# Sums over values for two heads in one TensorE stream, in a decoder layer on one core

## The chip, the core and the metric

The kernel runs on one core of one Trainium2 chip. A core has TensorE (PE: matmuls and transposes; its weight loads are shown as PEld), VectorE (DVE), ScalarE (ACT), GpSimd (POOL) and SyncE (SP, which here issues the DMA transfers). The metric is the device time of one execution in microseconds (us), lower is better.

## The reference

A decoder layer on x of 2 batches x 512 tokens x 1024. First, attention with 32 query heads, 8 key and value heads, head size 128, and a causal window of 128 keys; then a second mixing step with a quantised context of 2 x 1024 x 1024; then a feed-forward part with ternary weights. Each is added to x and normalised. The part that the change touches:

```python
def _gqa_swa_attention(q, k, v, slide):            # slide = 128
    qg = q.reshape(B, Hkv, G, N, D)                # G = 4 query heads for one k, v head
    s = jnp.einsum('bhgnd,bhmd->bhgnm', qg, k) * scale
    mask = (j <= i) & (i - j < slide)
    p = jax.nn.softmax(jnp.where(mask, s, -inf), axis=-1)
    return jnp.einsum('bhgnm,bhmd->bhgnd', p, v)   # the sums over values
...
o = attention(q, k, v); return o @ wo.T
```
and of the second step the quantised context: `clip(round(ctx / s + z), 0, 255)`.

## The kernel before, in words

All engines run hand-written streams, tied by semaphores. The first 437 us make q, k and v by fp32 products from pairs of values (high and low part, F32R), with three matmuls for each product: high by high, high by low, low by high. Then comes the **attention stage**, from 437 to 1031 us. It has 64 **units**: unit (g, j) is group g (0 to 7, one k and v head), batch j // 4 and query head j % 4, so a group has 8 units, j = 0 to 7. Work goes in **slots**, one for each unit. In slot j every engine runs its `slot_of(g, j)`:

- PE: `scores` of unit j; half of an output product (`out_slot(.., 0, ..)`, 12 matmuls of 512 columns); `values` of unit j - 2; `turn_probs` of unit j - 1 (transposes of the probabilities through PSUM bank 4, `turn_ps`); the second output product. At the end of slots 0 and 4 `turn_values` transposes the values of a batch, through the same bank.
- ACT: copies scores out of PSUM, `query_high` for the next unit, the exponentials, `sums_high(j - 2)` (the sums out of PSUM, rounded to the high part), `probs_high(j - 1)` (the same for the transposed probabilities), and once a slot `make_tile`, which prepares a weight tile of the feed-forward part.
- DVE: `softmax_bias(j)`, the add of the first output product, `check_tile`, `normalise(j)`, `sums_low(j - 2)`, `probs_low(j - 1)`, the add of the second output product.
- POOL: `query_low(j + 1)`, then `mask_probs(j - 1)`: four instructions that write the masked probabilities `pm_h` and `pm_l`, which `values` reads two PE slots after the unit's own.
- SP: loads of q, k, v, output weights, tiles and context, in program order.

A window of 128 keys means that key block a (128 keys) serves query blocks a and a + 1. So `values` has for each a three matmuls of 256 columns, and of 128 for the last block: 12 in a unit. They accumulate in one bank, `o_ps` (bank 5), with the weights `v_h`, `v_l`. Four banks (`y_ps`: 0, 1, 6, 7) take the output products in turn.

`contexts(g, j, ...)` says in which slots a context tile is scaled (ACT, line 1556), rounded (DVE, line 2477) and quantised (ACT, line 1562, in the next slot). The raw tile has two buffers in `ctx_raw`. After the last slot a tail follows: `out_tile`, sums of the context, a normalisation of eight row tiles, then the feed-forward part from about 1100 us.

Of the kernel before, what the change touches and what calls it, by code (L numbers as in the profile page):

```python
# [15 lines left out]
P = 128  # L16
# [8 lines left out]
KCTX = 1024  # L25
# [45 lines left out]
def build(nc, x_rows, x_cols, w_att, ctx_rows, x1_scale, x1_zp, x2_scale, x2_zp, w_gu, w_down, out):  # L71
    with ExitStack() as stack:
# [57 lines left out]
        pm_h = place("pm_h", [P, TPB, 2, P], F32R)  # L130
        pm_l = place("pm_l", [P, TPB, 2, P], F32R)
# [34 lines left out]
        ctx_raw = place("ctx_raw", [P, 2, KCTX], F32, at_r4 + 32768)  # L166
# [79 lines left out]
        y_ps = [bank(0), bank(1), bank(6), bank(7)]  # L246
# [277 lines left out]
        def out_block(j, k, last):  # L524
# [5 lines left out]
            return 0, 0, 2 * (j - 6) + k, 0  # L530

# [149 lines left out]
        def _(sp):  # L681
# [103 lines left out]
            def load_context(k, odd):  # L785
                if isinstance(k, int):
                    wait(sp, ctx_quant, k - 1)
                sp.dma_start(ctx_raw[:, odd, :], ctx_rows[k]).then_inc(ctx_loaded[odd], 16)

            def slot(g, j, first, last):  # L790
# [20 lines left out]
                if not first and j in (0, 2):  # L811
                    if last:
                        for odd in range(2):
                            load_context(2 * (HKV - 2) + j + odd, odd)
                    else:
                        load_context(g * 2 + (j // 2 - 2), j // 2)
# [153 lines left out]
        def _(pe):  # L970
# [79 lines left out]
            def values(g, j):  # L1050
# [5 lines left out]
                for a in range(TPB):  # L1056
# [4 lines left out]
                    ph = pm_h[:, a, 0:wide, :]  # L1061
                    pl = pm_l[:, a, 0:wide, :]
# [4 lines left out]
                last.then_inc(pv_done, 1)  # L1067

# [7 lines left out]
            def out_product(m, into, t, half):  # L1076

                wait(pe, y_added, m - 3)
# [9 lines left out]
            def out_slot(g, j, k, last):  # L1088
# [12 lines left out]
                out_product(g * 16 + (2 * j + k - 12), y_ps[(2 * j + k) % 4], t, half)  # L1101

            def out_tile(t):
# [3 lines left out]
                for half in range(NH):  # L1107
                    m = OUT_BLOCKS - 2 * (TILES - t) + half
                    pe.wait_ge(y_added, m - 1)
                    out_product(m, y_ps[2 + half], t, half)  # L1110

            def slot_of(g, j, first, last):
                early = first and j < 6
                scores(g, j)
                if early:
# [10 lines left out]
                if j % GROUP == 0:  # L1126
                    turn_values(g, j // GROUP)
# [98 lines left out]
            values(g, 6)  # L1226
# [4 lines left out]
            values(g, 7)  # L1231
# [201 lines left out]
        def _(act):  # L1433
# [95 lines left out]

            def head_high(n, e):  # L1530
# [22 lines left out]
            def scale_context(k, odd, loads):  # L1553

                act.wait_ge(ctx_loaded[odd], loads * 16)
                act.activation(ctx_raw[:, odd, :], ctx_raw[:, odd, :], ACT.Relu,
# [1503 lines left out]
```

## Time and profile before

| | |
|---|---|
| median of 3 runs | 1482.17 us (1480.92 to 1483.05) |
| profiled execution, whole | 1483.74 us |
| its span, first to last instruction | 1481.6 us |
| PE busy in the span | 1439.5 us (97%) |
| DVE / ACT / POOL busy | 984.0 / 788.8 / 739.9 us |
| PE busy, 437 to 1031 us (attention) | 586.57 of 594 us |
| granted TensorE clock in that stretch | 1.00 |

The span is the profiler's; the whole is the device time of the same execution, 2.1 us more. PE matmuls overlap: the time that one takes of the engine is the distance between its start and the next one's, not its own duration.

### The profile page before, as it was taken

The numbers are of one execution on the slowest core, as the hardware profiler recorded it, in microseconds if no ns is written. First come the engines' busy times: TensorE is split into PE (matmuls) and PEld (weight loads), VectorE is DVE, ScalarE is ACT, GpSimd is POOL, SyncE is SP. The second block draws the span as 40 slices with busy tenths as digits, with TensorE's granted clock in tenths as the row PEclk, the third lists the DMA queues.
The fourth block names the chain that finished last, engine by engine and source line by source line (L and its number), as shares of the span: only waits on it lengthen the run. The fifth ranks groups of instructions, "written<-read, shape, count | busy, mean of one in ns | idle before, by whom it ended". The sixth has DMA issues, their size and how long they took to land.

```text
span 1481.6 us, 23450 instructions
## 1 busy us (share of the span) xinstructions
PE 1439.5 (97%) x7349; PEld 1174.3 (79%) x7349; DVE 984.0 (66%) x1768; ACT 788.8 (53%) x1561; POOL 739.9 (50%) x651
## 2 busy tenths in 40 slices
PE   8899999999999999999999999999989999999996
PEld 6688888888888888888888888887757887777643
DVE  7644444445556578777777877787776665566587
ACT  5433333333445465656565756674576555555674
POOL 0477777776566455555555455553475434433100
PEclk9999999999999999999999999999999999999999
DMA  6477777877662857575757676772041222222611
GB/s 227 156 273 272 275 283 283 281 275 256 222 222 79 300 184 263 179 272 191 279 184 262 216 244 227 248 230 98 16 156 71 93 86 78 90 92 85 228 43 73
DMA packets 105883, 281.12 MB, mean 190 GB/s; under 512 B 12768, under 2 KB 13152, under 8 KB 105824
## 3 DMA queue, kind: packets, MB, share of 16 engines
q1 hardware_dynamic: 105824, 280.41, 53.9%
q8 instruction: 28, 0.46, 0.1%
q14 instruction: 31, 0.25, 0.1%
HBM read 184.94 MB, written 95.42 MB: 189 GB/s over the span
## 4 chain that ended last, share of the span: by engine, by line
PE 52%; DVE 7%; ACT 3%; DMA 3%; issue 3%; POOL 2%; SPq 1%; DVEq 0%; ACTq 0%; POOLq 0%
PE ps L1083 7%; PE ps L1084 7%; PE ps L1085 7%; PE ps L1246 6%; PE ps L1247 6%; PE ps L1299 5%; PE ps L1034 2%; PE ps L1035 2%; PE ps L1036 2%; PE ps L1065 2%; PE ps L1066 2%; PE ps L1047 2%; PE ps L1064 1%; PE ps L1168 1%; DVE u_val L2761 1%
## 5 line engine op out<-in xcount | busy, mean ns | idle before, releaser
L1015 PE MATMUL ps<-xo_h,wb_h 128*128 128x512 f32 x644 | 251.4, 390 | 6.5 <-DVE xo_l L2323 2.8
L1016 PE MATMUL ps<-xo_l,wb_h 128*128 128x512 f32 x644 | 250.7, 389 | 0.0
L1017 PE MATMUL ps<-xo_h,wb_l 128*128 128x512 f32 x644 | 250.6, 389 | 0.0
L2098 POOL TENSOR_TENSOR pm_l<-pt_l,upto 128x512 fp32r<-128x512 f32 x64 | 82.4, 1288 | 251.8 <-DVE pt_l L2422 251.8
L1083 PE MATMUL ps<-wo_h,o_h 128*128 128x512 f32 x512 | 206.4, 403 | 0.0
L1084 PE MATMUL ps<-wo_l,o_h 128*128 128x512 f32 x512 | 199.8, 390 | 0.0
L1085 PE MATMUL ps<-wo_h,o_l 128*128 128x512 f32 x512 | 199.6, 390 | 0.0
L1459 ACT ACTIVATE wb_h<-wf_l 128x512 fp32r<-128x512 f32 x69 | 43.6, 632 | 197.1 <-DVE wf_l L2351 81.7
L1015 PEld LDWEIGHTS ps<-xo_h,wb_h 128*128 128x128 f32 x644 | 120.9, 188 | 34.6 <-issue 5.9
L2071 POOL TENSOR_TENSOR wb_l<-wf_l,wb_h 128x512 fp32r<-128x512 f32 x66 | 87.7, 1329 | 112.0 <-DVE s_sum L2346 56.6
L1508 ACT ACTIVATE prob<-prob,exp_bias 128x128 f32<-128x128 f32 x256 | 99.8, 391 | 78.4 <-DVE exp_bias L2409 78.4
L1017 PEld LDWEIGHTS ps<-xo_h,wb_l 128*128 128x128 f32 x644 | 120.9, 188 | 25.2
L1016 PEld LDWEIGHTS ps<-xo_l,wb_h 128*128 128x128 f32 x644 | 120.9, 188 | 24.5
L2071 POOL TENSOR_TENSOR wb_l<-raw,wb_h 128x512 fp32r<-128x512 f32 x66 | 89.0, 1349 | 62.1 <-DVE wb_l L2335 47.5
L2432 DVE TENSOR_TENSOR resid<-ps,resid 128x512 f32<-128x512 f32 x128 | 88.3, 690 | 47.3 <-PE ps L1085 43.0
L1085 PEld LDWEIGHTS ps<-wo_h,o_l 128*128 128x128 f32 x512 | 96.1, 188 | 21.3
L1083 PEld LDWEIGHTS ps<-wo_h,o_h 128*128 128x128 f32 x512 | 96.5, 188 | 16.6
L1084 PEld LDWEIGHTS ps<-wo_l,o_h 128*128 128x128 f32 x512 | 96.6, 189 | 15.8
L2087 POOL TENSOR_TENSOR q_l<-q_raw,q_h 128x512 fp32r<-128x512 f32 x64 | 83.6, 1307 | 21.5 <-ACT q_h L1486 21.5
L1246 PE MATMUL ps<-t_h,ws 128*128 128x512 f32 x228 | 88.7, 389 | 0.0
L1247 PE MATMUL ps<-t_l,ws 128*128 128x512 f32 x228 | 88.7, 389 | 0.0
L2082 POOL TENSOR_TENSOR wp_l<-wp_raw,wp_h 128x1024 fp32r<-128x1024 f32 x32 | 76.8, 2399 | 0.0
(252 smaller groups left out, 3649.8 us busy)
## 6 DMA issues: line engine op xcount, KB each, us to landing
raw<-w_att SPq DMA_DIRECT2D x47, 512.0 KB, 5.6
f_raw<-w_gu SPq DMA_DIRECT2D x44, 512.0 KB, 4.8
u_gu<-f_unit SPq DMA_DIRECT2D x42, 512.0 KB, 4.4
gq<-u_gu SPq DMA_DIRECT2D x42, 512.0 KB, 3.7
wp_raw<-w_att SPq DMA_DIRECT2D x32, 512.0 KB, 5.7
wo_high<-wp_h SPq DMA_DIRECT2D x32, 512.0 KB, 2.9
wo_low<-wp_l SPq DMA_DIRECT2D x32, 512.0 KB, 4.2
q_rows<-c SPq DMA_DIRECT2D x64, 256.0 KB, 2.7
```

What stands on the lines that cost most here:

```text
L1015: pe.matmul(prod_ps[i], wh, chunk(xo_h[i], c), start=(i in OPENS and c == 0), stop=False, skip_group_check=True)
L1016: pe.matmul(prod_ps[i], wh, chunk(xo_l[i], c), start=False, stop=False, skip_group_check=True)
L1017: last = pe.matmul(prod_ps[i], wl, chunk(xo_h[i], c), start=False, stop=(c == KH - 1), skip_group_check=True)
L1083: pe.matmul(into, oh, wo_h[half][:, h, :], start=(h == 0), stop=False)
L1084: pe.matmul(into, oh, wo_l[half][:, h, :], start=False, stop=False)
L1085: last = pe.matmul(into, ol, wo_h[half][:, h, :], start=False, stop=(h == GROUP - 1))
L1246: pe.matmul(dst, w[:, c * P:(c + 1) * P], chunk(xh, c), start=(start and c == 0), stop=False, skip_group_check=True)
L1247: last = pe.matmul(dst, w[:, c * P:(c + 1) * P], chunk(xl, c), start=False, stop=(c == KH - 1), skip_group_check=True)
L1508: last = act.activation(prob[:, par, a, :], prob[:, par, a, :], ACT.Exp, bias=exp_bias[:, par, a:a + 1], scale=SCALE, accum_out=row_sum[:, ...
L2071: pool.tensor_tensor(wb_l[i][:, :], weight_source(odd, i), plain(wb_h[i][:, :]), ALU.subtract).then_inc(w_low, 1)
L2087: pool.tensor_tensor(q_l[:, j % 2, :], q_raw[:, :], plain(q_h[:, j % 2, :]), ALU.subtract).then_inc(q_low, 1)
L2432: dve.tensor_tensor(resid[:, t, cols], source, resid[:, t, cols], ALU.add).then_inc(y_added, 1)
```

## The change

`values` is kept for the first six units of group 0. From then on `values_pair(g, j - 3)` runs in odd slots alone and does units j - 3 and j - 2 (always two heads of one batch, with the same values) with one set of weights: one matmul streams the masked probabilities of both heads. The pair's sums need two banks, 5 and 1 (`oq_ps`, each 2 heads x 256 columns). So the output products have three banks in turn instead of four. `pm_h` and `pm_l` get room for two units. `sums_high_pair` and `sums_low_pair` take the two banks one after another, 2 x 256 columns each. `turn_values` moves from the end of slots 0 and 4 to behind the scores of slots 1 and 5, and `value_high` and `value_low` with it. `ctx_raw` has one buffer, whose next load waits for the quantising of the tile before; in the last group the four context tiles go to slots 1, 3, 5, 7 instead of 1 to 4. In the tail `values(g, 6)` and `values(g, 7)` become one `values_pair(g, 6)` at the later place.

```diff
+        oq_ps = [bank(i).rearrange("p (h k) -> p h k", h=2) for i in (5, 1)]
+        y_ps = [bank(0), bank(6), bank(7)]
+        Y_BANK = (0, 1, 2, 0, 1, 2, 0, 1, 2, 0, 1, 2, 0, 1, 2, 1)
...
-            if last and 1 <= j <= 4:
-                k = 2 * (HKV - 2) + j - 1
+            if last and j > 0 and j % 2 == 1:
+                k = 2 * (HKV - 2) + j // 2
...
             def load_context(k, odd):
-                if isinstance(k, int):
-                    wait(sp, ctx_quant, k - 1)
-                sp.dma_start(ctx_raw[:, odd, :], ctx_rows[k]).then_inc(ctx_loaded[odd], 16)
+                wait(sp, ctx_quant, k)
+                sp.dma_start(ctx_raw[:, :], ctx_rows[k]).then_inc(ctx_loaded[odd], 16)
...
+            def values_pair(g, j):
+                n = g * UNITS + j
+                par, b, h = unit(j)
+                pe.wait_ge(p_masked, n + 2)
+                wait(pe, o_low, n)
+                def into(dst, a, first, wide, start, stop):
+                    vh = v_h[b][:, a, :]
+                    vl = v_l[b][:, a, :]
+                    ph = pm_h[:, :, a, first:first + wide, :]
+                    pl = pm_l[:, :, a, first:first + wide, :]
+                    pe.matmul(dst, vh, ph, start=start, stop=False, skip_group_check=True)
+                    pe.matmul(dst, vh, pl, start=False, stop=False, skip_group_check=True)
+                    return pe.matmul(dst, vl, ph, start=False, stop=stop, skip_group_check=True)
+                low, high = oq_ps
+                into(low[:, :, 0:2 * P], 0, 0, 2, True, False)
+                into(low[:, :, P:2 * P], 1, 0, 1, False, True).then_inc(pv_done, 1)
+                into(high[:, :, 0:P], 1, 1, 1, True, False)
+                into(high[:, :, 0:2 * P], 2, 0, 2, False, False)
+                into(high[:, :, P:2 * P], 3, 0, 1, False, True).then_inc(pv_done, 1)
...
                 scores(g, j)
+                if j % GROUP == 1:
+                    turn_values(g, j // GROUP)
...
-                if not first or j >= 2:
+                if first and j >= 2:
                     values(g, j - 2)
+                if not first and j % 2 == 1:
+                    values_pair(g, j - 3)
...
-                if j % GROUP == 0:
-                    turn_values(g, j // GROUP)
...
+            def sums_high_pair(g, j):
...
+                for i in range(2):
+                    act.wait_ge(pv_done, n + (i + 1))
+                    act.activation(o_h[b][:, h:h + 2, i * 2 * P:(i + 1) * 2 * P], oq_ps[i], ACT.Copy).then_inc(o_high, 1)
```

The order in which the instructions stand shows three places. First, PE, the sums over values in a slot of the last group before the change, the end of one unit's (line 1064 to 1066 are high by high, low by high, high by low) and the transposes of the probabilities:

```order
L1064 MATMUL ps<-pm_h,v_h_81 128x256
L1065 MATMUL ps<-pm_l,v_h_81 128x256
L1066 MATMUL ps<-pm_h,v_l_82 128x256
L1064 MATMUL ps<-pm_h,v_h_81 128x128
L1065 MATMUL ps<-pm_l,v_h_81 128x128
L1066 MATMUL ps<-pm_h,v_l_82 128x128
L1047 MATMUL ps<-ident,prob 128x128 x4
```
and of the changed kernel the beginning of a pair's in an odd slot (three more of 128x2x128 follow, then the transposes; 128x2x128 is a stream of 256 columns in two pieces):

```order
L1094 MATMUL ps<-pm_h,v_h_81 128x512
L1095 MATMUL ps<-pm_l,v_h_81 128x512
L1096 MATMUL ps<-pm_h,v_l_82 128x512
L1094 MATMUL ps<-pm_h,v_h_81 128x2x128
L1095 MATMUL ps<-pm_l,v_h_81 128x2x128
L1096 MATMUL ps<-pm_h,v_l_82 128x2x128
L1094 MATMUL ps<-pm_h,v_h_81 128x2x128
L1095 MATMUL ps<-pm_l,v_h_81 128x2x128
L1096 MATMUL ps<-pm_h,v_l_82 128x2x128
L1094 MATMUL ps<-pm_h,v_h_81 128x512
L1095 MATMUL ps<-pm_l,v_h_81 128x512
L1096 MATMUL ps<-pm_h,v_l_82 128x512
```
A pair has 15 matmuls (6 of 512 columns, 9 of 256) where two units had 24 (18 of 256, 6 of 128), and an even slot has none.

Second, PE at the border of slots 4 and 5, before:

```order
L1084 MATMUL ps<-wo_l_155,o_h_149 128x512
L1085 MATMUL ps<-wo_h_153,o_l_151 128x512
L1070 REGISTER_ALU
L1073 MATMUL ps<-ident,v_raw 128x128 x4
L1024 REGISTER_ALU
L1034 MATMUL ps<-k_h_143,q_h 128x128
```
and now, in slot 5:

```order
L1047 MATMUL ps<-k_h_142,q_h 128x256
L1048 MATMUL ps<-k_l_143,q_h 128x256
L1049 MATMUL ps<-k_h_142,q_l 128x256
L1106 REGISTER_ALU
L1109 MATMUL ps<-ident,v_raw 128x128 x4
L68 REGISTER_ALU
L1118 MATMUL ps<-wo_h_152,o_h_148 128x512
```
The transposes of the values moved from ahead of the scores to behind them.

Third, DVE in slot 5 of the last group, before:

```order
L2407 TENSOR_REDUCE row_max<-prob 128x4
L2409 TENSOR_SCALAR exp_bias<-row_max 128x4
L2432 TENSOR_TENSOR resid<-ps,resid 128x512
L2461 TENSOR_TENSOR misfits<-misfits 128x1
L2471 SCALAR_TENSOR_TENSOR f_raw_161,misfits<-f_unit_165,prm,f_raw_161 128x1024
L2415 RECIPROCAL row_inv<-row_sum 128x4
L2417 TENSOR_TENSOR prob<-prob,row_inv 128x512
L2427 TENSOR_TENSOR o_l_151<-ps,o_h_149 128x512
L2422 TENSOR_TENSOR pt_l<-ps,pt_h 128x512
L2432 TENSOR_TENSOR resid<-ps,resid 128x512
```
and now:

```order
L2465 TENSOR_REDUCE row_max<-prob 128x4
L2467 TENSOR_SCALAR exp_bias<-row_max 128x4
L2452 TENSOR_TENSOR v_l_145<-ps,v_h_144 128x512
L2499 TENSOR_TENSOR resid<-ps,resid 128x512
L2528 TENSOR_TENSOR misfits<-misfits 128x1
L2538 SCALAR_TENSOR_TENSOR f_raw_162,misfits<-f_unit_166,prm,f_raw_162 128x1024
L2473 RECIPROCAL row_inv<-row_sum 128x4
L2475 TENSOR_TENSOR prob<-prob,row_inv 128x512
L2493 TENSOR_TENSOR o_l_149<-ps,o_h_147 128x2x256 x2
L2480 TENSOR_TENSOR pt_l<-ps,pt_h 128x512
L2499 TENSOR_TENSOR resid<-ps,resid 128x512
```
The low part of the values came into this slot, and the odd slot has both takings of the sums; the even slots have none ahead of `pt_l`.

## Rows read from the trace of the kernel before

**Rows 1.** Page, part 1: busy time, share, instructions of PE.
```profile
PE 1439.5 (97%) x7349; PEld 1174.3 (79%) x7349; DVE 984.0 (66%) x1768; ACT 788.8 (53%) x1561; POOL 739.9 (50%) x651
```

**Rows 2.** Windows, attention stage: length, busy PE, PEld, DVE, ACT, POOL; clock, DMA, GB/s.
```profile
437.00:1031.00 594.00, 586.57 (x3478) 515.41 (x3477) 449.41 (x885) 355.02 (x903) 308.86 (x345) 1.00 0.63 218
```

**Rows 3.** Waits of PE, 456 to 1031 us: total, times, longest.
```profile
PE ps L1073 <- DVE pt_l L2422: 4.7, 5, 1.6
PE ps L1034 <- POOL q_l L2087: 0.8, 1, 0.8
PE ps L1064 <- POOL pm_l L2103: 0.6, 2, 0.3
```

**Rows 4.** Timeline of PE, one slot (group 3, slot 6): start, duration.
```profile
783.18 0.22 PE L1034 MATMUL ps<-k_h,q_h 128*128 128x128 f32 x1
...
784.59 0.40 PE L1083 MATMUL ps<-wo_h,o_h 128*128 128x512 f32 x1
...
787.33 0.28 PE L1064 MATMUL ps<-pm_h,v_h 128*128 128x256 f32 x1
...
788.40 0.22 PE L1064 MATMUL ps<-pm_h,v_h 128*128 128x128 f32 x1
...
788.69 0.62 PE L1047 MATMUL ps<-ident,prob 128*128 128x128 f32 x4
789.07 0.48 PE L1083 MATMUL ps<-wo_h,o_h 128*128 128x512 f32 x1
...
791.89 0.22 PE L1034 MATMUL ps<-k_h,q_h 128*128 128x128 f32 x1
```

**Rows 5.** Timeline of PE, value transposes: one without, and the three longest waits.
```profile
774.03 0.60 PE L1073 MATMUL ps<-ident,v_raw 128*128 128x128 f32 x4
774.38 0.31 PE L1034 MATMUL ps<-k_h,q_h 128*128 128x128 f32 x1
...
488.31 0.63 PE L1073 MATMUL ps<-ident,v_raw 128*128 128x128 f32 x4 [1.64 <-DVE pt_l L2422]
...
526.40 0.63 PE L1073 MATMUL ps<-ident,v_raw 128*128 128x128 f32 x4 [1.53 <-DVE pt_l L2422]
...
987.59 0.63 PE L1073 MATMUL ps<-ident,v_raw 128*128 128x128 f32 x4 [0.94 <-DVE pt_l L2422]
```

**Rows 6.** Timeline of DVE, the same slot as rows 4, from its merging of scores on.
```profile
785.51 0.58 DVE L2403 COPY_PREDICATED prob<-later,ps 128x384 f32<-128x384 uint32 x1
...
789.62 0.69 DVE L2417 TENSOR_TENSOR prob<-prob,row_inv 128x512 f32<-128x512 f32 x1
790.23 0.68 DVE L2427 TENSOR_TENSOR o_l<-ps,o_h 128x512 fp32r<-128x512 f32 x1
790.83 0.68 DVE L2422 TENSOR_TENSOR pt_l<-ps,pt_h 128x512 fp32r<-128x512 f32 x1
792.09 0.69 DVE L2432 TENSOR_TENSOR resid<-ps,resid 128x512 f32<-128x512 f32 x1 [0.58 <-PE ps L1085]
```

**Rows 7.** Timeline of POOL: low part of q, masks; then masks of a tight slot.
```profile
785.88 1.29 POOL L2087 TENSOR_TENSOR q_l<-q_raw,q_h 128x512 fp32r<-128x512 f32 x1 [0.18 <-ACT q_h L1486]
...
791.59 1.29 POOL L2098 TENSOR_TENSOR pm_l<-pt_l,upto 128x512 fp32r<-128x512 f32 x1 [4.42 <-DVE pt_l L2422]
...
793.89 0.52 POOL L2103 TENSOR_SCALAR_AFFINE_SELECT pm_l<-pt_l 128x384 fp32r<-128x384 f32 x1
...
971.52 0.52 POOL L2103 TENSOR_SCALAR_AFFINE_SELECT pm_l<-pt_l 128x384 fp32r<-128x384 f32 x1
```

**Rows 8.** Timeline of PE: sums over values behind the masks of rows 7.
```profile
796.05 0.28 PE L1064 MATMUL ps<-pm_h,v_h 128*128 128x256 f32 x1
...
973.21 0.28 PE L1064 MATMUL ps<-pm_h,v_h 128*128 128x256 f32 x1
```

**Rows 9.** Timeline of ACT: tiles that came late by DMA.
```profile
783.60 1.15 ACT L1551 ACTIVATE f_unit<-f_raw,prm 128x1024 fp32r<-128x1024 f32 x1 [2.34 <-DMA f_raw<-w_gu]
```

**Rows 10.** Timeline of DVE: a context tile's rounding.
```profile
990.02 0.87 DVE L2477 TENSOR_SCALAR ctx_raw<-ctx_raw 128x1024 f32<-128x1024 f32 x1 [0.44 <-ACT ctx_raw L1556]
```

More of the change, by code:

```diff
@@ L129, in build @@
         pt_l = place("pt_l", [P, TPB, P], F32R)
-        pm_h = place("pm_h", [P, TPB, 2, P], F32R)
-        pm_l = place("pm_l", [P, TPB, 2, P], F32R)
+        at_pm = at[0]
+        pm_h = place("pm_h", [P, 2, TPB, 2, P], F32R)
         s2_sum = place("s2_sum", [P, SEQ], F32)
@@ L165, in build @@
         ctx_q = place("ctx_q", [P, BATCH * KC, KCTX], BF16, at_r4)
-        ctx_raw = place("ctx_raw", [P, 2, KCTX], F32, at_r4 + 32768)
+        ctx_raw = place("ctx_raw", [P, KCTX], F32, at_r4 + 32768)
+        pm_e = place("pm_e", [P, TPB, 2, P], F32R, at_pm + 4096)
+        pm_l = place("pm_l", [P, 2, TPB, 2, P], F32R, at_r4 + 36864)
         at_t = xo_at[PS3]
@@ L530, in out_block, with y_turn, y_since @@
             return 0, 0, 2 * (j - 6) + k, 0
+        SINGLES = 6
+        def y_turn(j, k):
+            return (2 * j + k + 4) % 16
+        def y_since(j, k):
+            turn = y_turn(j, k)
+            return next(d for d in range(1, 16) if Y_BANK[(turn - d) % 16] == Y_BANK[turn])
         def late_product(event):
@@ L810, in slot @@
                         sp.dma_start(param(i), source.rearrange("(a b) -> a b", a=1).to_broadcast([P, 1])).then_inc(prm_loaded, 16)
[L811 to L816, printed above, removed]
+                if last and j % 2 == 0:
+                    k = 2 * (HKV - 2) + j // 2
+                    load_context(k, k % 2)
+                if not first and not last and j in (0, 2):
+                    load_context(g * 2 + (j // 2 - 2), j // 2)
                 tiles_slot(g, j, first, last)
@@ L1100, in out_slot @@
                     pe.wait_ge(wo_loaded[1], g * 32 + 32)
-                out_product(g * 16 + (2 * j + k - 12), y_ps[(2 * j + k) % 4], t, half)
+                m = g * 16 + (2 * j + k - 12)
+                wait(pe, y_added, g * 16 + (2 * j + k - 11 - y_since(j, k)))
+                out_product(m, y_ps[Y_BANK[y_turn(j, k)]], t, half)
             def out_tile(t):
@@ L1230, in _ @@
             out_tile(3)
-            values(g, 7)
+            values_pair(g, 6)
             slot(2)
@@ L1555, in scale_context @@
                 act.wait_ge(ctx_loaded[odd], loads * 16)
-                act.activation(ctx_raw[:, odd, :], ctx_raw[:, odd, :], ACT.Relu,
+                act.activation(ctx_raw[:, :], ctx_raw[:, :], ACT.Relu,
                                bias=param(Z2), scale=param(R2)).then_inc(ctx_scaled, 1)
@@ L1581, in slot_of @@
                     late(event)
-                if not first or j >= 2:
+                if first and j >= 2:
                     sums_high(g, j - 2)
+                if not first and j % 2 == 1:
+                    sums_high_pair(g, j - 3)
                 if first and j == 1:
@@ L1812, in _ @@
             g = HKV - 1
+            for k, odd, loads in contexts(g, UNITS - 1, False, True):
+                quantise_context(k, odd)
             slot(0)
-            sums_high(g, 6)
             probs_high(g, 7)
             slot(1)
-            sums_high(g, 7)
+            sums_high_pair(g, 6)
             for i in range(2, FIRST_SLOT):
@@ L2427, in sums_low, with sums_low_pair @@
                 dve.tensor_tensor(o_l[b][:, h, :], o_ps, plain(o_h[b][:, h, :]), ALU.subtract).then_inc(o_low, 1)
+            def sums_low_pair(g, j):
+                n = g * UNITS + j
+                par, b, h = unit(j)
+                for i in range(2):
+                    rows = slice(i * 2 * P, (i + 1) * 2 * P)
+                    dve.wait_ge(o_high, n + (i + 1))
+                    dve.tensor_tensor(o_l[b][:, h:h + 2, rows], oq_ps[i], plain(o_h[b][:, h:h + 2, rows]),
+                                      ALU.subtract).then_inc(o_low, 1)
             def add_product(m, source, t, half):
@@ L2496, in slot_of @@
                     late(event)
-                if not first or j >= 2:
+                if first and j >= 2:
                     sums_low(g, j - 2)
+                if not first and j % 2 == 1:
+                    sums_low_pair(g, j - 3)
                 if not first or j >= 1:
```

48 lines of the change are left out of this document (28 added, 20 removed).

## The prediction

> **What bounds the kernel now.** I read the busy shares first: PE is busy for 1439.5 of 1481.6 us [rows 1], so the question is what the change does to PE's stream and to its waits. The windows by stage say that in the attention stage, where the whole change lies, PE is busy for 586.57 of 594 us at the full granted clock, while DVE has 449 and POOL 309 [rows 2]. The list of PE's waits in this stage has three rows, 6.1 us together [rows 3]. The rest is the stream itself, so I read one slot of it in the timeline [rows 4]: it begins at 783.18, the next at 791.89, 8.71 us, with no idle time in it. What PE spends is the distance from start to start. The scores take 1.41 us (783.18 to 784.59), the first output product 2.74 us for 12 streams of 512 columns (0.228 each), the sums over values 1.36 us: nine streams of 256 columns in 1.07 (787.33 to 788.40, 0.119 each) and three of 128 in 0.29 (to 788.69, 0.097 each); the four transposes 0.38, the second output product 2.82.
>
> **The streams.** Two units took 2 x 1.36 = 2.72 us. A pair has 6 streams of 512 and 9 of 256 columns: 6 x 0.228 + 9 x 0.119 = 2.44 us, 0.28 less. The columns are the same (5376); what goes is nine streams' extra and the poor rate of the 128-column ones. Pairs: four in each of groups 1 to 7 and one in the tail, 29; **29 x 0.28 = 8.1 us**. No row shows a stream that is read in two pieces. From below it costs as a stream of its width in one piece (0.119 and 0.228). From above it costs as two streams of the piece's width: 2 x 0.097 = 0.193 for 256 columns, 2 x 0.119 = 0.238 for 512, so 3.17 us a pair. I take the lower, since a piece boundary changes one address within a stream, and a stream of 256 in one piece is the nearest row; the other end is a rival below. If only the 512s cost twice a 256, the pair is 2.50 and the term 6.5 us.
> TensorE's page in the Trainium skill, "TensorE: Matmul & The Clock Gate" (section Back-to-back issue gap), gives the isolated gap as N/2.4 + 2.5 ns. By it nine streams fewer save only 9 x 2.5 = 22.5 ns a pair, 0.65 us in all, and the time would be about 1478; the rows here have 12 ns over the columns' own time at 256 and 15 at 512, and the trace does not agree with 2.5.
>
> **The value transposes.** They wait for `pt_l` of the unit before, 4.7 us in five places [rows 3, 5]. Behind the scores they come 1.41 us later. At 488.31 (group 0, slots of the old form) 1.64 becomes 0.23. In slot 0 of a later group PE comes to the next slot 1.36 us sooner (no sums there), the scores give 1.41 back, and DVE's `pt_l` comes 0.60 sooner, since `o_l` no longer stands ahead of it [rows 6]: the wait shrinks by 0.65. So 1.53 becomes 0.9 and 0.94 becomes 0.3; the two not shown (0.6 together, from the total) go. Together 4.7 becomes 1.4 us: **3.3 us gained**, all 4.7 at best, none if DVE slips. Undisturbed, the transposes cost 0.35 [rows 5] at either place. Streams of 128 are no longer ahead of the probability transposes (0.38 there [rows 4], 0.35 behind a 512 [rows 5]): 58 x 0.03 is 1.7 at most; I take **0.5**.
>
> **The masks, which the pair waits for.** Here is the thin place. The pair in an odd slot needs the mask of the unit that was transposed in the even slot before. Now: `pt_l` ends at 791.51, 8.33 into the slot [rows 4, 6], POOL masks from 791.59 to 794.41 (2.82 us) [rows 7], and the sums start at 796.05: 1.64 us to spare [rows 8]. After: the even slot is 8.71 - 1.36 = 7.35 us and the sums start 4.15 into the next, so 11.50 instead of 12.86; `pt_l` ends 0.60 sooner, the masks at 11.23 - 0.60 = 10.63. To spare: 0.87 us. In the tightest odd slot, 971.52 + 0.52 = 972.04 against 973.21, 1.17 us become 0.4 [rows 7, 8]. In slots 1 and 5 the value transposes lie before the pair now and were after the sums before, with nothing lost. So no wait on average; I charge **0.4 us** for the odd late one. If this cover is gone, every pair waits for the excess, and behind it stand the probability transposes and both banks.
> In odd slots the pair's second bank is done at 4.15 + 2.44 = 6.6; ACT and DVE each take it in 0.6, so `pt_l` ends near 9.2, in a slot of 9.8, and its mask is needed a slot and a half later. `v_l` (0.6) and `v_h` (0.6) ahead of normalising in slots 1 and 5 lie in the same time. The shorter even slot does not hold up the next scores: those of this slot are merged 2.9 us into it (785.51 + 0.58) [rows 6].
>
> **Banks.** An output product now waits for the add of the third one before it (at two of 16 turns the second before) where it was the fourth. DVE adds a slot's second product at 792.09 to 792.78, 0.9 into the next slot [rows 6]; the product that needs the bank soonest is that slot's second, 4.5 us into it. Nothing.
>
> **DMA and the context.** SP's wait for the quantised tile (slot 2) is over before the q load ahead of it may go (that waits for `q_low`, which ends 4.0 us into the slot [rows 7], and ACT quantises before 4). Nothing. Tiles that come late hold ACT now and then: 783.60 is 0.4 into slot 6 and its tile ends just as the scores do [rows 9]. The two slots before are 0.28 us shorter, so ACT's copy slips by some 0.3 there, and with it the mask of that slot: 0.87 becomes about 0.5. In the last group slots 4 and 6 get a context load of 512 KB each beside the output weights, a further 1 to 2 us for the tile: this may cost up to 1 us once; in exchange slot 2 has one load less to wait for. I take 0 for both.
>
> **Tail.** Slot 7 has a context tile more: 0.87 us on DVE at most [rows 10] and two ACT passes about as long as a tile's, 1.15 [rows 9]. PE needs the first add of the tail only two output products later (2 x 2.74 [rows 4]), and the quantised tile later still. Nothing; 1.5 us at worst, where the normalisation of the first row tile starts that much later.
>
> **Sum.** 8.1 + 3.3 + 0.5 - 0.4 = 11.5 us. The profiled execution took 1483.74 (span 1481.6 and 2.1 around it), so 1472.2 for it, and against the median of the runs, 1482.17, **1470.7 us**. After the stage the feed-forward part begins when the rows are there, so what PE gains passes on.
>
> **Rivals.**
> A, *masks late in part* (18 in 100). If POOL or DVE is later than worked out by 0.5 us more than the spare 0.87 leaves, each pair waits: 0.1 to 0.3 us in 29 pairs is 3 to 8 us, and the time 1474 to 1479. For it: DVE is busy for 449 of 594 us and the slots' waits for tiles [rows 9]; against it: the same chain held 1.64 us now with `o_l` in it.
> B, *only columns count* (4). The streams take the columns' time whatever their number, the gain is that of the transposes, 3.3: 1478.9. Against it: the 128-column streams take 0.097, not half of 0.119 [rows 4]. The page's N/2.4 + 2.5 ns gives nearly this, 0.65 us more gain.
> C, *slower: a stream in two pieces costs two* (4). Place: the 15 streams of each pair. 3.17 instead of 2.72, 29 x 0.45 = 13.0 us lost, less 3.3 + 0.5: 9.2 slower, 1491. It decides from 0.165 us for a two-piece stream of 256 columns on: with 512s at 0.228 a pair is then 1.37 + 1.48 = 2.85, 0.13 more than now, and 29 x 0.13 uses up the 3.8 us of the transposes. Against it: nothing in the rows but their silence.
> D, *tile or tail lateness* (8). DMA-late tiles in slots 5 and 7 and the longer tail take 2 to 6 us of the gain: 1473 to 1477.
> E, *the masks miss by far* (3). More than 1.25 us late, each pair waits 0.4: no gain or a loss, 1480 to 1488.
> F, more gain than worked out (5): all waits of the transposes and all borders, 1467.
>
> **How the numbers follow.** The forecast (faster by 9 to 14 us, 1468 to 1473) has 58 in 100. From it the range goes down to 1467.5 (all of the 4.7 and half the borders) and up through D and most of A to 1477; what is left out is B, C, E, the end of A and half of F. A measurement tells 0.2%, 3.0 us, from no change. Faster by more: forecast, A, D, F and part of B, 0.91; within: rest of B, part of E, 0.04; slower: C and part of E, 0.05.
>
> **What would show it.** In the profile after: two-piece streams at a distance of 0.12 us, 512s at 0.228, a pair of 2.44; odd plus even slot 17.14 us instead of 17.42; PE's wait at the value transposes 1 to 2 us; little or no wait of the pair for `pm_l`. Wrong if the list of PE's waits has `pm_l` with more than 2 us, if the pair's streams are farther apart, or if the tail from PE's last slot to the feed-forward part is longer than before.

## The result and the profile after

The changed kernel takes **1473.93 us** (median of 5 runs, 1472.15 to 1474.61) where the kernel before takes 1482.17 (5 runs beside it, 1480.92 to 1485.54): a ratio of 0.994, 95% interval 0.9928 to 0.9951, 8.2 us faster. In a second series the same code took 1473.63 against 1482.11. The forecast was 1470.7, in a range of 1467.5 to 1477.0; it was 3.2 us too low. The gain of 8.2 us lies below the 9 to 14 that had 58 in 100.

The page, part 1, of the kernel after, and its window over most of the attention stage (columns as in [rows 1, 2]):

```profile
PE 1431.7 (97%) x7072; PEld 1158.4 (79%) x7088; DVE 1002.9 (68%) x1768; ACT 791.0 (54%) x1561; POOL 740.1 (50%) x651
...
437.00:1022.00 585.00, 579.28 (x3222) 499.87 (x3222) 467.45 (x884) 357.76 (x904) 310.36 (x346) 1.00 0.64 221
```

PE is busy for 7.8 us less. DVE is busy for 19 us more with as many instructions (1768); that comes back below. The stage, from the first scores to the first transposes of the quantised tile behind it, went from 594.07 us (437.64 to 1031.71) to 584.26 (438.72 to 1022.98): 9.8 less. PE's waits in it (total, times, longest), to be read against [rows 3]:

```profile
PE ps L1118 <- DMA wo_l<-wo_low: 1.8, 2, 1.1
...
PE ps L1109 <- DVE pt_l L2480: 1.2, 2, 1.0
PE ps L1047 <- POOL q_l L2137: 0.8, 1, 0.8
PE ps L1077 <- POOL pm_e L2161: 0.3, 1, 0.3
```

The value transposes (now line 1109) wait for 1.2 us in place of 4.7. The pair (line 1094) has no row: it never waits for its masks. New is the first row: twice PE waits for output weights (the line is that of `out_product`). A pair in PE's timeline (start, duration; the last line joins four transposes):

```profile
772.90 0.39 PE L1094 MATMUL ps<-pm_h,v_h 128*128 128x512 f32 x1
773.13 0.39 PE L1095 MATMUL ps<-pm_l,v_h 128*128 128x512 f32 x1
...
773.58 0.28 PE L1094 MATMUL ps<-pm_h,v_h 128*128 128x256 f32 x1
773.69 0.28 PE L1095 MATMUL ps<-pm_l,v_h 128*128 128x256 f32 x1
...
774.29 0.40 PE L1094 MATMUL ps<-pm_h,v_h 128*128 128x512 f32 x1
...
775.35 0.60 PE L1060 MATMUL ps<-ident,prob 128*128 128x128 f32 x4
```

From start to start a stream of 512 columns takes 0.23 us and one of 256 takes 0.11 to 0.12, though each is read in two pieces (one for each head). The pair takes 775.35 - 772.90 = 2.45 us, forecast 2.44.

The thin place was the mask. The last mask instruction on POOL and the pair that needs it, in slot 3, then in slot 7 of group 4:

```profile
753.90 0.52 POOL L2161 TENSOR_SCALAR_AFFINE_SELECT pm_l<-pt_l 128x384 fp32r<-128x384 f32 x1
...
789.41 0.52 POOL L2161 TENSOR_SCALAR_AFFINE_SELECT pm_l<-pt_l 128x384 fp32r<-128x384 f32 x1
```
```profile
755.30 0.39 PE L1094 MATMUL ps<-pm_h,v_h 128*128 128x512 f32 x1
...
790.05 0.44 PE L1094 MATMUL ps<-pm_h,v_h 128*128 128x512 f32 x1
```

To spare are 755.30 - 754.42 = 0.88 us (forecast 0.87) and 790.05 - 789.93 = 0.12. The second follows a slot in which ACT had waited 3.67 us for a feed-forward tile:

```profile
780.30 1.16 ACT L1598 ACTIVATE f_unit<-f_raw,prm 128x1024 fp32r<-128x1024 f32 x1 [3.67 <-DMA f_raw<-w_gu]
```

That slot begins at 778.53. (The slot of [rows 4] is slot 6 of group 4, groups counted from 0, not of group 3 as written there; nothing hangs on it.)

The two new waits, and the issue of the second transfer on SP's queue:

```profile
517.83 0.49 PE L1118 MATMUL ps<-wo_h,o_h 128*128 128x512 f32 x1 [0.79 <-DMA wo_l<-wo_low]
...
997.24 0.50 PE L1118 MATMUL ps<-wo_h,o_h 128*128 128x512 f32 x1 [1.06 <-DMA wo_l<-wo_low]
```
```profile
987.87 0.51 SPq L757 DMA_DIRECT2D wo_l<-wo_low  x1
```

For later use, the length of a group (its eight slots, from the first scores of one group to those of the next) as worked out from PE's timeline; groups 3 to 6 of a kernel ("regular" groups in what follows) agree within 0.05 us except where more is said:

| kernel | group 0 | group 1 | groups 3 to 6 |
|---|---|---|---|
| before | 78.36 | 72.30 | 70.65 (once 71.12) |
| move of the value transposes alone | 77.21 | 71.73 | 70.59 |
| after, single streams | 76.98 | 72.70 | 70.79 |
| after | 76.76 | 71.65 | 69.49 (69.63 and 69.68 in groups 4 and 5) |
| after, transposes moved back | 77.82 | 72.36 | 71.12 |
| after, weights first | 77.73 | 73.96 | 69.50 |
| after, mask 0.63 us longer | 76.83 | 74.22 | 71.35 to 71.79 |
| the same, weights first | 76.53 | 74.09 | 70.62 |
| after, 1.3 us of POOL behind the mask | 76.41 | 73.51 | 71.88 to 72.47 |

### The profile page after: what moved, and what is told of

Read it like the earlier page. It is cut to its first block, busy times and chain, and to the rows that moved or that the text cites. A ratio compares the mean times of both kernels' runs of the same rounds, so it can differ in the third digit from the quotient of the medians.

```text
span 1472.5 us, 22884 instructions
## 1 busy us (share of the span) xinstructions
PE 1431.7 (97%) x7072; PEld 1158.4 (79%) x7088; DVE 1002.9 (68%) x1768; ACT 791.0 (54%) x1561; POOL 740.1 (50%) x651
## 4 chain that ended last, share of the span: by engine, by line
PE 54%; DVE 6%; ACT 3%; issue 2%; DMA 2%; POOL 1%; SPq 1%; DVEq 0%; ACTq 0%; POOLq 0%
PE ps L1118 8%; PE ps L1120 7%; PE ps L1119 7%; PE ps L1284 6%; PE ps L1285 6%; PE ps L1337 5%; PE ps L1048 2%; PE ps L1047 2%; PE ps L1049 2%; PE ps L1060 2%; PE ps L1095 2%; PE ps L1094 2%; PE ps L1096 2%; PE ps L1207 1%; DVE u_val L2829 1%
## 5 line engine op out<-in xcount | busy, mean ns | idle before, releaser
L2156 POOL TENSOR_TENSOR pm_l<-pt_l,upto 128x512 fp32r<-128x512 f32 x58 | 74.8, 1290 | 230.4 <-DVE pt_l L2480 230.4
```

## Experiments

### Both parts of the gain, one at a time

**Single streams.** The pair's place, masks and banks stay, but the matmuls are the 24 of two units.

```diff
-                    ph = pm_h[:, :, a, first:first + wide, :]
-                    pl = pm_l[:, :, a, first:first + wide, :]
...
+                for i in range(2):
+                    for a in range(TPB):
...
+                        dst = bank((5, 1)[i])[:, a * P:(a + wide) * P]
...
+                        ph = pm_h[:, i, a, 0:wide, :]
+                        pl = pm_l[:, i, a, 0:wide, :]
```

> The changed kernel, but each head of a pair with its own streams in its own bank: 24 matmuls a pair (18 of 256 columns, 6 of 128) as before the change; slots, three product banks, masks and value transposes as in the changed kernel. Theory S (the streams' distances give the gain): a pair takes 2.72 us instead of 2.45, so 29 x 0.27 = 8 us more than the changed kernel, about 1482, and only the transposes' saving of some 2 us is left against before. Rival T (pairing pays by the order of slots or by the halved number of handovers): 1474 to 1477.

Measured: 1482.19 us (1480.81 to 1486.02), ratio to before 1.0003 (0.9994 to 1.0012). Without the streams' part the whole gain is gone; it was 8.3 us. An odd slot is 10.12 us where it is 9.79 with pairs. That is 0.33 and not the 0.27 of the two units' streams: where the second unit's first stream of 256 columns follows the first unit's last of 128, it takes 0.17 us (777.55 to 777.72) in place of 0.12.

**Value transposes back at the end of slots 0 and 4**, the rest as in after.

```diff
                 scores(g, j)
-                if j % GROUP == 1:
-                    turn_values(g, j // GROUP)
...
                     out_slot(g, j, 1, last)
+                if j % GROUP == 0:
+                    turn_values(g, j // GROUP)
```

> The changed kernel, but the value transposes (and the taking of their high and low parts) at the end of slots 0 and 4 again. Theory S: an even slot is 1.36 us shorter, the low part of the probabilities comes only 0.60 us sooner, so the transposes that had 0.4 us to spare before now wait about 0.4 us in each of 14 places, and the long waits get longer: 7 to 9 us of waits, 1480 to 1482; the move is then what pairing needs. Rival: the waits of the transposes are an accident of a few slots and pairing does not change them: 3 us of waits, 1476 to 1478.

Measured: 1484.75 us (1482.81 to 1489.12), ratio 1.0025 (1.0014 to 1.0036), more than the 1480 to 1482 expected, with more waits than the 7 to 9 us. PE's waits, first row:

```profile
PE ps L1109 <- DVE pt_l L2480: 11.9, 15, 2.1
```

**The move alone**, in the kernel before.

```diff
+                if j % GROUP == 1:
+                    turn_values(g, j // GROUP)
...
-                if j % GROUP == 0:
-                    turn_values(g, j // GROUP)
```

> The kernel before, with the value transposes moved behind the scores of slots 1 and 5 and nothing else. Theory S: the waits of 4.7 us shrink to about 1 (in the full-length slots the transposes come 1.41 us later): 3.5 us faster, 1478 to 1479. Rival: what is waited for there is waited for at the next step (sums or probability transposes): no gain, 1482.

Measured: 1479.59 us (1478.51 to 1480.41), ratio 0.9984 (0.9975 to 0.9993): 2.2 us faster, not 3.5. Its waits:

```profile
PE ps L1083 <- DMA wo_l<-wo_low: 1.2, 2, 0.7
...
PE ps L1073 <- DVE pt_l L2422: 0.4, 2, 0.2
```

The three together: in the kernel before, the move is worth 2.2 us by the medians (1481.74 to 1479.59), and 0.06 us in a regular group, so it lies in the few long waits. With pairs it is worth 10.8 us (1484.75 to 1473.93), since in a short even slot the transposes at its end wait for `pt_l` each time (15 times, 11.9 us). The move isn't a gain beside the pairing but its condition. The pairing itself is 70.59 - 69.49 = 1.1 us a group, 0.27 a pair. And waits for output weights stand already in the kernel with the move alone, at the same two products: 0.48 us at the first product of group 1 (517.28) and 0.72 in slot 7 of the last group (1004.61). With the transposes moved back the first of them is gone and the second is 0.34.

### The banks

**Three product banks in the kernel before**, with their waits as in after.

```diff
-        y_ps = [bank(0), bank(1), bank(6), bank(7)]
+        y_ps = [bank(0), bank(6), bank(7)]
+        Y_BANK = (0, 1, 2, 0, 1, 2, 0, 1, 2, 0, 1, 2, 0, 1, 2, 1)
```

> The kernel before with three banks for the output products in the changed kernel's turn, bank 1 idle, nothing else. Theory S: no new wait of PE, 1482 as before. Rival (the bank taken away costs a part of what pairing gives): waits of the output products for the adds, 1 to 3 us slower.

Measured: 1481.58 us (1480.72 to 1482.60), ratio 0.9995 (0.9985 to 1.0004), no new row among PE's waits, and regular groups of 70.65 us, as before. Giving up the fourth bank costs nothing.

### The wait for output weights

**The last group's context loads behind the tile's.**

```diff
+                if not first and not last and j in (0, 2):
+                    load_context(g * 2 + (j // 2 - 2), j // 2)
+                tiles_slot(g, j, first, last)
                 if last and j % 2 == 0:
                     k = 2 * (HKV - 2) + j // 2
                     load_context(k, k % 2)
-                if not first and not last and j in (0, 2):
-                    load_context(g * 2 + (j // 2 - 2), j // 2)
-                tiles_slot(g, j, first, last)
```

> The changed kernel; in the last group the context load stands behind the tile's store and load of its slot, no longer ahead of them. Theory D (the context load in slot 6 competes with the output weights that slot 7 waits for): the wait for wo_l in slot 7, 1.06 us, goes or halves; 0.5 to 1 us faster than the changed kernel. Rival (the wait comes from the shorter slot 6 alone: the weights are asked for 1.36 us later relative to their use): the wait stays at about 1 us and the time is the same.

Measured: 1472.47 us (1471.56 to 1475.66), ratio 0.9931 (0.9917 to 0.9944). This interval and that of after overlap almost wholly. The waits stay, and that of the last group is 1.57 us (1.06 in the kernel after):

```profile
PE ps L1118 <- DMA wo_l<-wo_low: 2.3, 2, 1.6
```

**The last two context tiles loaded to 128 of 1024 columns** (this leaves part of the context out).

```diff
-                sp.dma_start(ctx_raw[:, :], ctx_rows[k])
+                cols = slice(0, P if isinstance(k, int) and k >= 2 * HKV - 2 else KCTX)
+                sp.dma_start(ctx_raw[:, cols], ctx_rows[k][:, cols])
```

> The changed kernel; the last two context tiles are loaded with 128 of their 1024 columns, so 64 KB instead of 512 KB each (the rest of the tile is left as it was, so those rows of the quantised context are wrong). Theory D: no wait for wo_l in slot 7 of the last group. Rival (shorter slot alone): a wait of 0.7 us or more stays.

Measured once: 1473.6 us. The waits:

```profile
PE ps L1119 <- DMA wo_l<-wo_low: 1.5, 2, 1.1
```
```profile
517.40 0.49 PE L1119 MATMUL ps<-wo_h,o_h 128*128 128x512 f32 x1 [1.12 <-DMA wo_l<-wo_low]
996.39 0.50 PE L1119 MATMUL ps<-wo_h,o_h 128*128 128x512 f32 x1 [0.40 <-DMA wo_l<-wo_low]
```

The row must be read by place. The long wait is that of group 1, which this edit doesn't touch. The one in the last group, for which the edit was made, is 0.40 us, where it is 1.06 and 1.36 in the two profiles of the kernel after. So neither expectation holds (none, or 0.7 and more): the wait shrank but stayed. It is one profile, and how long these weights take to land varies. From their issue on SP's queue to the last landing, as worked out from the trace's DMA events, it is 8.67 us here, 9.33 and 9.64 in the kernel after and 9.84 with the context load behind, but 8.62 and 8.86 in the two kernels with transposes moved back and with single streams, which load the whole context tile at the same place. How much of the wait the context load makes, nothing up to some 1 us, stays open.

**Weights first**, beside **the changed kernel again** on the same chip.

```diff
+                if j in (4, 6):
+                    load_out(g, j // 2 - 2)
                 if not (last and j + 2 >= UNITS):
                     load_query(g, j + 2)
...
-                if j == 4:
-                    load_out(g, 0)
-                if j == 6:
-                    load_out(g, 1)
```

> The changed kernel with the two weight loads of slots 4 and 6 issued at the start of their slots, ahead of the query's load, not behind it. Theory W (the new waits for wo_l come from the weights' load, which is issued too late for a slot that is 0.3 us shorter for each stream): the load of group 0 lands earlier, and the wait of 0.8 us at the first slot of group 1 goes; in the last group the load of slot 6 lands up to 1 us earlier and the wait of 1.06 us in slot 7 shrinks by as much. About 1 us less than the changed kernel, 1472 to 1473 us, with wo_l waits of 0 to 1.0 us. Rival V (both weights wait for a low part that ScalarE or the chain behind the landing makes, or for their buffer, so that an earlier issue does nothing): wo_l stays at 1.8 us in 2, and the time stays at 1474.

> The changed kernel unchanged, on the chip of the three others, so that they have its time beside theirs. From its runs so far 1472.2 to 1474.6 us. The waits of TensorE in the value stage should be those of its first profile: wo_l about 1.8, pt_l about 1.2, and none for pm_l in the pair streams. If they vary by over 0.5 us from profile to profile, differences of that size between the other runs tell nothing.

Measured: 1475.41 us (1474.21 to 1476.69), ratio 0.9955 (0.9942 to 0.9969), against 1473.63 (1471.60 to 1474.56), ratio 0.9939 (0.9925 to 0.9953), for the changed kernel again, whose waits were `wo_l` 2.4, `pt_l` 1.3 and none for `pm_l` in the pairs. PE's waits with the weights first:

```profile
PE ps L1107 <- DVE pt_l L2478: 2.7, 2, 2.5
PE ps L1045 <- POOL q_l L2135: 1.8, 2, 1.0
```

and ACT's for the query of group 1, with the weights first, then in the kernel after:

```profile
513.13 0.63 ACT L1522 ACTIVATE q_h<-q_raw 128x512 fp32r<-128x512 f32 x1 [5.54 <-DMA q_raw<-q_rows]
```
```profile
512.44 0.63 ACT L1524 ACTIVATE q_h<-q_raw 128x512 fp32r<-128x512 f32 x1 [3.58 <-DMA q_raw<-q_rows]
```

Theory W was right in that both waits for `wo_l` are gone, and wrong on the time: 1.8 us more than the kernel beside it by the medians, with ranges that overlap by 0.4, and not 1 us less. The query that the weights passed lands later, ACT stands 5.54 us for it, and behind ACT come `q_l` (1.0 us at 515.36) and `pt_l` (2.5 us at 527.10). Group 1 takes 73.96 us in place of 71.65. The transfers at the seam of groups 0 and 1 are simply late; their order only decides who waits. In slot 6 of the last group no query is loaded, so the edit moves nothing ahead there: the second transfer is issued 0.61 us into the slot as before, but lands in 7.55 us. Moving the weights in the last group alone was not tried.

### What the spare of the masks is worth

**A mask longer by one POOL instruction**, of 1.29 us (a product of `pt_l` into a free tile) and, in another kernel, of 0.63 us (a selection of `pt_h`).

```diff
+                if not (isinstance(g, int) and g == 0 and j <= SINGLES):
+                    pool.tensor_tensor(qt(s2_sum[:, :]), pt_l[:, :, :].bitcast(F32),
+                                       upto[:, :].unsqueeze(1).to_broadcast([P, TPB, P]), ALU.mult)
```
```diff
+                if not (isinstance(g, int) and g == 0 and j <= SINGLES):
+                    pool.affine_select(out=qt(s2_sum[:, :]), in_=pt_h[:, :, :].bitcast(F32), compare_op=ALU.is_ge,
+                                       fill=0.0, base=0, pattern=[[0, TPB], [1, P]], channel_multiplier=-1)
```

> The changed kernel with one more instruction of 1.29 us on GpSimd in each mask (a product written to a tile that nobody reads). Theory S: 0.88 us are to spare in slots 3 and 7, some 0.5 in slot 1, 1.3 in slot 5, so PE waits 0.4 in 14 slots and 0.7 in 7: 9 to 12 us of waits for pm_l, 1483 to 1486. Rival (GpSimd's masks are hidden with more room than the first read says, or the wait is made up for elsewhere): under 3 us, 1474 to 1477.

> The changed kernel with one more instruction of 0.63 us on GpSimd in each mask. Theory S: within what is to spare in most slots; slot 1 of some groups and the two slots with 0.1 and 0.3 us to spare wait: 1 to 2 us of waits for pm_l, 1475 to 1476. Rival (masks already on the edge): 6 us and more, 1480.

Measured: with 1.29 us 1508.62 (1507.96 to 1509.91), ratio 1.0185 (1.0170 to 1.0201); with 0.63 us 1486.63 (1486.16 to 1488.75), ratio 1.0029 (1.0017 to 1.0042). That is 34.7 and 12.7 us over the changed kernel, where direct lateness gave 9 to 12 and 1 to 2. PE's waits, for the mask of 1.29, then of 0.63 us more:

```profile
PE ps L1094 <- POOL pm_l L2164: 22.2, 27, 1.7
PE ps L1109 <- DVE pt_l L2483: 6.5, 7, 1.3
```
```profile
PE ps L1094 <- POOL pm_l L2164: 7.7, 12, 1.7
PE ps L1109 <- DVE pt_l L2483: 3.0, 8, 1.0
```

A wait of 1.7 us behind a mask that is 0.63 us longer and had 0.12 to 0.88 to spare: something doubled the delay. A place in the first of them, where POOL's low part of the query comes just as DVE checks a tile:

```profile
604.59 1.28 POOL L2137 TENSOR_TENSOR q_l<-q_raw,q_h 128x512 fp32r<-128x512 f32 x1
```
```profile
604.63 2.33 DVE L2541 SCALAR_TENSOR_TENSOR f_raw<-f_unit,prm,f_raw 128x1024 f32<-128x1024 f32 x1
```

The check takes 2.33 us, against 1.27 where POOL is idle (784.33 in the kernel after). So two theories were on the table: POOL and DVE lengthen one another (P), or the transfers are late (T), since SP's load of the next query waits for `q_low` and the tile's load stands behind it.

**The 1.3 us of POOL behind the mask's signal.** The mask is neither longer nor, by this, later; only `q_l` is.

```diff
                 last.then_inc(p_masked, 1)
+                if not (isinstance(g, int) and g == 0 and j <= SINGLES):
+                    wait(pool, again, g * UNITS + (j - SINGLES - 1))
+                    pool.tensor_tensor(qt(s2_sum[:, :]), upto[:, :].unsqueeze(1).to_broadcast([P, TPB, P]),
+                                       upto[:, :].unsqueeze(1).to_broadcast([P, TPB, P]), ALU.mult).then_inc(again, 1)
```

> The changed kernel with a further POOL instruction of about 1.3 us behind each mask's signal: the mask itself is no longer and starts no later by its own length, only what POOL does next (the low part of the query) comes 1.3 us later. Theory P (the low part of the query then meets DVE's check_tile, which takes 2.3 us in place of 1.27 while POOL works, so that pt_l and with it the next mask are late): TensorE waits 5 to 15 us for pm_l and 3 to 6 us for pt_l, check_tile's mean rises over 1.4 us, and the time is 1480 to 1500 us. Rival D (in the two mask experiments only the mask's own length made the pair streams wait): POOL has over 1.3 us of idle time a slot, so nothing waits for pm_l, and the time is that of the changed kernel within 1 us, plus what q_l makes the scores wait (0.8 us before, 2 us at most).

Measured: 1490.97 us (1488.94 to 1491.67), ratio 1.0060 (1.0046 to 1.0074), 17.3 over the changed kernel beside it. The Rival D of this expectation is out. PE's waits, and a place on POOL and DVE:

```profile
PE ps L1110 <- DVE pt_l L2485: 8.9, 15, 0.9
PE ps L1095 <- POOL pm_l L2162: 4.5, 6, 1.1
PE ps L1119 <- DMA wo_l<-wo_low: 2.9, 2, 2.0
```
```profile
779.96 1.30 POOL L2138 TENSOR_TENSOR q_l<-q_raw,q_h 128x512 fp32r<-128x512 f32 x1
780.26 1.01 DVE L2533 TENSOR_TENSOR misfits<-misfits 128x1 f32<-128x1 f32 x1
781.20 1.27 DVE L2543 SCALAR_TENSOR_TENSOR f_raw<-f_unit,prm,f_raw 128x1024 f32<-128x1024 f32 x1
```

An add of one column, 0.14 us when alone, takes 1.01 and ends at 781.27; POOL's instruction ends at 781.26. DVE's instruction did not run slowly, it stood until POOL's was over. Over the stage this add has (count, busy, mean ns), in this kernel and in the kernel after:

```profile
L2533 DVE TENSOR_TENSOR misfits<-misfits 128x1 f32<-128x1 f32 x58 | 43.1, 743 | 3.1 <-ACT f_down L1599 3.1
```
```profile
L2528 DVE TENSOR_TENSOR misfits<-misfits 128x1 f32<-128x1 f32 x58 | 18.2, 315 | 3.4 <-ACT f_down L1598 3.4
```

The Trainium skill says it in "SBUF — State Buffer" (section SBUF: two separate sides): VectorE and GpSimd share a pair of ports, which is held whole by the one that starts first, so that the other blocks; of VectorE's instructions this holds for those in a 2-port performance mode and, against a GpSimd instruction that reads SBUF, for those with two inputs in SBUF. The add has two inputs in SBUF and POOL's `q_l` reads there, and the two ends at 781.26 and 781.27 agree with a lock and not with a shared rate.

**The mask of 0.63 us more, with the weights first**: it moves the transfers and leaves POOL and DVE their work.

```diff
+                if j in (4, 6):
+                    load_out(g, j // 2 - 2)
...
+                    pool.affine_select(out=qt(s2_sum[:, :]), in_=pt_h[:, :, :].bitcast(F32), compare_op=ALU.is_ge,
+                                       fill=0.0, base=0, pattern=[[0, TPB], [1, P]], channel_multiplier=-1)
```

> The two edits together: a further POOL instruction of 0.63 us in each mask, and the weight loads of slots 4 and 6 first. The mask's 0.63 us alone cost 12.7 us over the changed kernel. Theory T (what makes it cost so much is the tile that is loaded behind these transfers in slot 7, and ScalarE's wait of 4.4 us for it): with the loads moved the masks of slot 7 are on time again, and the time falls to about 1478 us. Theory P (POOL's and DVE's instructions lengthen one another where they meet, whenever the transfers land): the order of the loads changes little, 1485 to 1487 us, with some 7 us of waits for pm_l and a mean of check_tile on DVE over 1.4 us, as with the mask alone.

Measured: 1479.99 us (1478.33 to 1482.16), ratio 0.9986 (0.9977 to 0.9995): 6.4 over the changed kernel, not 12.7, and 4.6 over the one with the weights first. ACT's waits for tiles, with the longer mask alone, then with the weights first too:

```profile
ACT f_unit L1598 <- DMA f_raw<-w_gu: 27.5, 7, 5.0
ACT f_down L1598 <- DMA f_raw<-w_down: 9.2, 7, 2.7
```
```profile
ACT f_down L1596 <- DMA f_raw<-w_down: 2.5, 1, 2.5
```

From 36.7 us in 14 waits to 2.5 in one, while its waits for queries rose from 9.8 to 14.7 us. PE's waits, to be read against those with the longer mask alone:

```profile
PE ps L1107 <- DVE pt_l L2481: 5.7, 8, 2.5
...
PE ps L1092 <- POOL pm_l L2162: 0.9, 5, 0.2
```

The 7.7 us for `pm_l` have become 0.9, so slot 7, where the long ones stood, was held by late tiles: T is right there. P is right for the rest, since with the tiles on time slot 1 of a regular group is still 1.1 us longer than in the kernel after (11.35 against 10.23). What happens is seen in the slot before (of group 2), on POOL and DVE:

```profile
592.64 1.28 POOL L2135 TENSOR_TENSOR q_l<-q_raw,q_h 128x512 fp32r<-128x512 f32 x1
592.71 1.25 DVE L2468 TENSOR_SCALAR exp_bias<-row_max 128x4 f32<-128x4 f32 x1
```

`exp_bias`, for which ACT's exponentials wait, ends with POOL's instruction, 6.08 us into its slot (587.88 to 593.96). In the kernel after it took 0.66 us there and ended at 5.19. The transposed probabilities are 0.9 us later by it, and the value transposes wait for them. DVE's check of a tile has the same mean with the longer mask alone (1461 ns) and with the weights first (1462 ns), so it was not the check alone that mattered, as I had thought after the first mask runs.

## Why the prediction came out as it did

**Streams, 8.1 us: right.** A pair is 2.45 us for 2.44, an even and an odd slot without value transposes 7.37 + 9.79 = 17.16 for 17.14, and a regular group is 1.1 us shorter by the pairing: 0.27 x 29 = 7.8 us. A stream in two pieces costs no more than one in one piece, so rival C and the upper end of the term are out. So is rival B: with the same columns in 24 streams the gain was gone. The step on which this rests held: what a stream costs over its columns by [rows 4], 12 ns at 256 columns, 15 at 512 and 44 at 128. The 2.5 ns that the prediction named beside it, from the Trainium skill, "TensorE: Matmul & The Clock Gate" (section Back-to-back issue gap), would have given 0.65 us; the page states them for an isolated matmul, and these streams do not agree with them.

**Value transposes, 3.3 us: right.** 4.7 became 1.2 (1.64 became 0.23 at 489.71, 1.53 became 0.96 at 526.39).

**Borders, 0.5 us: not there.** The two slots shrink by 17.42 - 17.16 = 0.26, and the pair alone has 0.27 of it. That this term and the next, both wrong, cancel is luck.

**Masks, 0.4 us of loss: none.** The spare is 0.88 for 0.87 where the chain is undisturbed and 0.12 where a tile was late; 0.4 had been expected at the tightest. The prediction let a late tile cost the next mask some 0.3 us. It was more: the pass over the tile began 780.30 - 778.53 = 1.77 us into its slot, for 0.43 before [rows 4, 9]. The pair waited nowhere. The waits of the single sums for masks in the first group went from 0.6 us in two [rows 3] to 0.3 in one, another 0.3 gained.

**DMA, 0 us: the step that failed.** The prediction had "this may cost up to 1 us once" for the last group's context load and took 0. The waits for output weights cost 1.8 us in this profile, 2.4 in the second. They stand at two places, with two reasons.

At the first product of group 1 (517.83) PE simply arrives sooner. In the kernel before it came at 517.41, and the last of the weights had landed at 517.03, only 0.38 us ahead. The wait of 1.64 us at 488.31 is 0.23 now, and three slots later PE stands 0.48 us (move alone) to 0.79 us for the weights; with the transposes moved back this wait is gone. So a third to a half of the 1.41 us that the longest of the five waits gave back is paid again there.

In slot 7 of the last group it is the length of slot 6. In every one of these kernels SP issues the second transfer 0.61 us into slot 6; PE needs it 9.50 us later before (997.39 to 1006.89) and 8.31 later now (987.87 to 996.18), because the slot has no sums over values. The landing took 9.16 us before and 8.62 to 10.24 in the kernels with short even slots (7.55 and 7.62 in the two with the weights first): there was 0.35 us to spare, and 1.2 were taken. (In the move alone the slot has its old length and PE waits 0.72 us, since this landing took 10.34; its scatter is as large as the spare.) What the context load beside it adds is open, as said above; that the prediction named it alone, and took 0 for it, left out both of these reasons.

That was a cost to be put in: where a wait is removed or a slot shortened, the next thing that lands on that engine from outside has to be looked up. I looked up only what the change itself moved.

**The tail and the banks, 0 us: right.** From the end of the stage to the end of the span 449.9 us before, 449.5 after. The three banks alone measured 0.9995.

**The sum.** In the stage 7.8 + 3.5 + 0.3 - 1.8 = 9.8, which is the 594.07 - 584.26 of the two profiles, for 11.5. That is 1.7 us of the miss of 3.2. The rest lies outside: in these two executions the part ahead of the stage, whose code is the same, is 1.1 us longer (438.72 against 437.64; other profiles of the same code have 437.1 to 438.1), and the medians differ by 8.2 to 8.5 us where the stages differ by 9.8 and, in the second profile (437.79 to 1022.44), 9.4. Some 1 us between profile and median stays unexplained. The time lies where rival D had it (1473 to 1477), but not by D's mechanism: the tail is no longer, and no late tile held the pair.

**The rivals' prices.** Rival A didn't come, but its price was wrong by far: "each pair waits for the excess", 3 to 8 us for masks beyond the spare. The measured price of 0.63 us more in the mask, less than the 0.88 to spare in most slots, is 12.7 us, and that of 1.29 us, 0.4 beyond the spare, is 34.7. A late mask is not only late. POOL's `q_l` behind it is late too; SP's load of the next query waits for it, and with it every transfer queued behind, so tiles land later and hold ACT; and POOL's instructions now meet those of DVE that make `exp_bias` and with it the next mask. The forecast stood nearer to a cliff than its 18 in 100 for an end at 1474 to 1479 told.

What the share of each way is in the 34.7 us of the longer mask is open: only the 0.63 us case was run with the weights first (12.7 to 6.4 us), and in that case some 2 us of the 6.4 are the seam of groups 0 and 1, which the weights' move itself spoils (group 1: 74.09 us, and 73.96 with the weights first and no longer mask).

## What to carry to other kernels

When a change takes a wait from the bounding engine, list what that engine consumes next from a queue outside (here output weights, three slots later) and ask when it lands; a part of the gain is paid back there. Do the same where a stretch gets shorter between the issue of a transfer and its use. Price a late producer by the loop it stands in, not by its excess: if the same engine also frees the buffer on which the loads wait, 0.6 us can become 13. And before a shortening of streams, look at what was hidden behind the old length: here the value transposes had to move first, or they would have taken all of it back.

## What the runs showed of the hardware

An instruction of DVE that reads or writes SBUF beside one of POOL's can stand until POOL's ends: an add of 128x1 took 1.01 us for 0.14, ending at 781.27 with POOL's at 781.26; a `TENSOR_SCALAR` of 128x4 took 1.25 us, ending at 593.96 with POOL's at 593.92. It is so each time: in the attention stage of the kernel after, 58 of the 64 `exp_bias` instructions and 19 of the 58 of `misfits` take over 0.25 us, and each of these ends within 0.1 us of the end of an instruction on POOL (before 50 of 64 and 3 of 58). It goes the other way too: a mask instruction of 0.52 us took 1.50 beside DVE's check (589.07 in the kernel after). This is also, in the main, where DVE's 19 us more came from, with no instruction added: `exp_bias` has a mean of 593 ns for 418 before (64 times, 11.2 us), `misfits` 315 for 174 (58 times, 8.1 us). I had read every duration from rows as if it belonged to the instruction; on these two engines it belongs to the pair.

A moving operand read in two pieces of 128 or 256 columns costs TensorE what one in a single piece costs, 0.12 us for 256 and 0.23 for 512 columns at the full granted clock.
